# Planning of two sparse layers in fewer operations, with a subtraction moved to GpSimd and gathers issued in pairs

## The reference

```python
def _L1_ffn_ref(x, Wr, W1, b1, W2, b2):
    DIM, E, K, H = (256, 8, 2, 1024)
    x_flat = x.reshape(-1, dim)
    logits = x_flat @ Wr
    w, ind = jax.lax.top_k(logits, K)
    w = jax.nn.softmax(w, axis=-1)
    combine = jnp.einsum('tke,tk->te', jax.nn.one_hot(ind, E, dtype=x.dtype), w)
    def body(acc, params):
        W1e, b1e, W2e, b2e, ce = params
        h = jax.nn.gelu(x_flat @ W1e + b1e, approximate=False)
        y = h @ W2e + b2e
        return (acc + ce[:, None] * y, None)
```

## Time and profile before

| | us |
|---|---|
| median of three runs | 1571.42 (1568.8 to 1572.77) |
| profiled execution, whole | 1568.99 |
| its span, first to last instruction | 1567.2 |
| PE busy | 1324.8 (85%) |
| DVE busy | 962.4 (61%) |
| ACT busy | 860.1 (55%) |
| POOL busy | 708.6 (45%) |
| mean granted PE clock | 0.927 of full |
| first sparse layer, from the planning to its last tile | about 519 to 818 |
| second sparse layer | about 1029 to 1239 |

### The profile page before, as it was taken

One profiled execution on the slowest core, in us unless ns is written; L12 is line 12 of the kernel. 1 busy time (PEld: TensorE's weight loads), 2 busy tenths in 40 slices (PEclk: granted clock), 3 DMA queues, 4 the chain that ended last, 5 costly groups with the idle time before them and its releaser, 6 DMA issues.

```text
span 1567.2 us, 29388 instructions
## 1 busy us (share of the span) xinstructions
PE 1324.8 (85%) x9497; PEld 962.0 (61%) x9524; DVE 962.4 (61%) x2651; ACT 860.1 (55%) x1718; POOL 708.6 (45%) x835
## 2 busy tenths in 40 slices
PE   2899899997998499999999699849999388995985
PEld 1455489854566289999986366627887245664343
DVE  6789653426785643333338499575554277967787
ACT  2366854434786245555535388535554155885554
POOL 4567330105632577767641473158994415622000
PEclk9999999997899699999999699969999797997998
DMA  9997030179640333343248974024444498710001
GB/s 291 280 159 145 2 98 0 37 226 194 120 77 15 101 124 120 116 158 112 79 146 275 213 135 84 13 86 151 146 135 162 150 277 166 138 33 1 0 14 41
DMA packets 115441, 188.86 MB, mean 121 GB/s; under 512 B 21169, under 2 KB 91441, under 8 KB 109105
## 3 DMA queue, kind: packets, MB, share of 16 engines
q0 software_dynamic: 36928, 105.19, 28.2%
q1 hardware_dynamic: 78368, 81.79, 16.9%
HBM read 128.17 MB, written 50.20 MB: 114 GB/s over the span
## 4 chain that ended last, share of the span: by engine, by line
PE 67%; DVE 14%; DMA 7%; ACT 6%; issue 4%; POOL 1%; ACTq 0%; SPq 0%; DVEq 0%; POOLq 0%
PE PS L1196 10%; PE PS L1216 10%; PE PS L1037 9%; PE PS L992 8%; PE PS L996 3%; PE PS L1208 3%; PE PS L1074 2%; DMA qk_parts<-q_parts 2%; PE PS L1010 2%; PE PS L878 2%; PE PS L1050 2%; PE PS L1017 2%; DMA stack<-qk_parts 1%; DVE act L2577 1%; PE PS L864 1%
## 5 line engine op out<-in xcount | busy, mean ns | idle before, releaser
L2092 DVE TENSOR_REDUCE nm<-PS 128x2 f32<-128x512 f32 x384 | 250.3, 676 | 42.6 <-PE PS L992 41.4
L992 PE MATMUL PS<-stack 48*128 48x256 f32 x1024 | 215.8, 336 | 43.6 <-DVE nm L2092 10.6
L992 PEld LDWEIGHTS PS<-stack 48*128 48x128 f32 x1024 | 154.5, 208 | 128.5 <-issue 59.1
L996 PE MATMUL PS<-stack 49*128 49x256 f32 x1024 | 206.0, 325 | 0.9 <-ACT probs L1517 0.6
L1216 PE MATMUL PS<-weights,hh 128*128 x936 | 190.0, 292 | 3.9 <-DVE hl L2419 3.7
L1196 PE MATMUL PS<-weights,xh 128*128 x468 | 171.1, 420 | 10.7 <-DVE xl L2403 5.2
L667 POOL DMA_DIRECT2D stack<-mt x128 | 72.8, 569 | 213.8 <-ACT mt L1526 211.8
L1517 ACT ACTIVATE probs<-PS 128x512 f32<-128x512 f32 x256 | 145.1, 595 | 42.9 <-PE PS L996 16.7
L1517 ACT ACTIVATE xng<-PS 128x512 f32<-128x512 f32 x256 | 145.2, 595 | 24.3 <-PE PS L1017 13.8
L1216 PEld LDWEIGHTS PS<-weights,hh 128*128 128x128 f32 x936 | 152.8, 193 | 6.3 <-issue 5.8
L996 PEld LDWEIGHTS PS<-stack 49*128 49x128 f32 x1024 | 145.5, 198 | 10.1 <-ACT probs L1517 4.3
(11 more groups left out here) (329 smaller groups left out, 3073.3 us busy)
## 6 DMA issues: line engine op xcount, KB each, us to landing
stack<-qk_parts POOLq DMA_DIRECT2D x128, 256.0 KB, 4.2
qk_parts<-stack SPq DMA_DIRECT2D x32, 512.0 KB, 6.9
qk_parts<-q_parts SPq DMA_DIRECT2D x32, 512.0 KB, 10.8
stack<-qk_parts POOLq DMA_DIRECT2D x128, 128.0 KB, 3.8
weights<-W_dram POOLq DMA_DIRECT2D x12, 1024.0 KB, 7.2
wide<-ctxT_dram SPq DMA_DIRECT2D x16, 512.0 KB, 8.1
wslot<-y_tokens SPq DMA_DIRECT2D x16, 512.0 KB, 7.6
weights<-W_dram POOLq DMA_DIRECT2D x12, 512.0 KB, 5.1
```

The costliest lines, as they stand in the source:

```text
L992: mm = pe.matmul(PS[:, u % 3, to], nat_q[:, at], nat_k, start=True, stop=True)
L996: mm = pe.matmul(PS[:, 3 + v % 3, to], key_k[:, at], key_q, start=(l > 0 or half == 0), stop=(l > 0), skip_group_check=(l == 0))
L2092: nc.vector.tensor_reduce(nm[:, j % 2, at:at + 2], PS[:, (2 * t + h) % 3, :].rearrange("p (q n) -> p q n", q=2), AX.X, ALU.max, negate=Tru ...
```

## The change

It makes five edits, in both sparse layers.

1. The two compares into `eq` become one over both choices, and so do the two multiplications by `where` and the two sums into `posf`. The semaphore counts (ROUTE + 2, PLANNED = 50) follow.
2. The eight chained operations on `tile_e` become one compare into `begun` (128 x 39 x 8, in the memory of `late`) and one sum over the eight experts.
3. `rows_of_tiles` is cut into `rows_from`, which writes `idx`, and `rows_to`, which writes `into`. For the first eight tiles `rows_to` is called after the tables.
4. The four pieces of `split_low(l, 1, q)` leave DVE. POOL does the same subtractions after its normalising and before it waits for `xt_out` and `idx_done`. Its last one adds to `split_done`.
5. Of the first eight gathers, 2 and 3 wait for the landing of 0 and 1; 4 waits for 2 and 3, and 6 for 4 and 5.

```diff
@@ gpsimd
                         normalise(2 * h)
                         normalise(2 * h + 1)
+                    for q in range(CUTS):
+                        at = slice(q * n // CUTS, (q + 1) * n // CUTS)
+                        pool.wait_ge(split_hi, SPLITS * (l - 1) + CUTS + q + 1)
+                        ins = nc.gpsimd.tensor_tensor(w_lo(l, 1)[:, at], w_raw(l, 1)[:, at], w_hi(l, 1)[:, at].bitcast(F32), ALU.subtract)
+                    pool.wait_ge(split_done, EXPERTS * (l - 1) + 1)
+                    ins.then_inc(split_done, 1)
                     pool.wait_ge(xt_out, 16 * GROUPS * l)
                     pool.wait_ge(idx_done, 2 * l - 1)
                     for i in range(AHEAD):
+                        if 2 <= i < 4:
+                            pool.wait_ge(xq_in[i - 2], 16 * l)
+                        elif i >= 4 and i % 2 == 0:
+                            pool.wait_ge(xq_in[i // 2], 32 * l)
                         gather(i, tile_in(i, i % 2)).then_inc(xq_in[i if i < 2 else 1 + i // 2], 16)
@@ tensor
-                pe.wait_ge(route_v[l], ROUTE + 3)
+                pe.wait_ge(route_v[l], ROUTE + 2)
@@ vector
-            def rows_of_tiles(l, k, first, part, block):
+            def rows_from(l, k, first, part, block):
...
                 nc.vector.scalar_tensor_tensor(idx[:, at], block, float(P), tmp(1), ALU.mult, ALU.add).then_inc(idx_done, 1)
+                return k + 2
+
+            def rows_to(l, k, first, part, block):
+
+                n = part.shape[1]
+                at = slice(first, first + n)
+                tmp = lambda r: scan[:, 0].rearrange("p t e -> p (t e)")[:, 32 * (r + 1):32 * (r + 1) + n]
                 nc.vector.scalar_tensor_tensor(tmp(2), block, 0.5, pad_row[:, at], ALU.is_lt, ALU.mult).then_inc(route_v[l], 1)
-                dve.wait_ge(route_v[l], k + 3)
-                tt(tmp(0), part, tmp(2), ALU.add).then_inc(route_v[l], 1)
-                dve.wait_ge(route_v[l], k + 4)
+                dve.wait_ge(route_v[l], k + 1)
+                nc.vector.tensor_tensor(tmp(0), part, tmp(2), ALU.add).then_inc(route_v[l], 1)
+                dve.wait_ge(route_v[l], k + 2)
                 nc.vector.scalar_tensor_tensor(into[:, at], block, float(P), tmp(0), ALU.mult, ALU.add).then_inc(placed, 1)
-                return k + 4
+                return k + 2
...
-                for m in range(2):
-                    nc.vector.tensor_tensor(eq[:, m], iotas[:, 0:8].unsqueeze(1).broadcast_to([P, TILES, 8]),
-                                            gt[:, m, :].unsqueeze(2).broadcast_to([P, TILES, 8]), ALU.is_equal
-                                            ).then_inc(route_v[l], 1)
-                k += 2
-                dve.wait_ge(route_v[l], k)
+                choices = eq[:].rearrange("p m t e -> p (m t) e")
+                then(tt(choices, iotas[:, 0:8].unsqueeze(1).broadcast_to([P, 2 * TILES, 8]),
+                        gt[:, 0:2, :].rearrange("p m t -> p (m t)").unsqueeze(2).broadcast_to([P, 2 * TILES, 8]), ALU.is_equal))
                 then(tt(picked[:], eq[:, 0], eq[:, 1], ALU.add))
...
-                for m in range(2):
-                    then(tt(eq[:, m], eq[:, m], where, ALU.mult))
-                    then(nc.vector.tensor_reduce(posf[:, m, :], eq[:, m], AX.X, ALU.add))
+                then(tt(eq[:], eq[:], where.unsqueeze(1).broadcast_to([P, 2, TILES, 8]), ALU.mult))
+                then(nc.vector.tensor_reduce(posf[:].rearrange("p m t -> p (m t)"), choices, AX.X, ALU.add))
...
-                k = rows_of_tiles(l, k, 0, PS[:, 6, 0:AHEAD], PS[:, 6, AHEAD:2 * AHEAD])
-                for e in range(8):
-                    if e == 0:
-                        then(ts(tile_e[:, 0, :], iotas[:, 0:NT], escan[:, es, 0:1], None, ALU.is_ge))
-                    else:
-                        then(nc.vector.scalar_tensor_tensor(tile_e[:, e % 2, :], iotas[:, 0:NT], escan[:, es, e:e + 1],
-                                                            tile_e[:, 1 - e % 2, :], ALU.is_ge, ALU.add))
+                k = rows_from(l, k, 0, PS[:, 6, 0:AHEAD], PS[:, 6, AHEAD:2 * AHEAD])
+                begun = late[:].rearrange("p i d -> p (i d)")[:, 0:8 * NT].rearrange("p (n e) -> p n e", e=8)
+                then(tt(begun, iotas[:, 0:NT].unsqueeze(2).broadcast_to([P, NT, 8]),
+                        upto.unsqueeze(1).broadcast_to([P, NT, 8]), ALU.is_ge))
+                then(nc.vector.tensor_reduce(tile_e[:, 1, :], begun, AX.X, ALU.add))
...
                 ts(upto_e[:], upto[0:1], 1.0 + (NT + 1) * (l - 1), None, ALU.add).then_inc(tables, 1)
+                k = rows_to(l, k, 0, PS[:, 6, 0:AHEAD], PS[:, 6, AHEAD:2 * AHEAD])
...
-                rows_of_tiles(l, k, AHEAD, PS[:, 7, 0:rest], PS[:, 7, rest:2 * rest])
+                k = rows_from(l, k, AHEAD, PS[:, 7, 0:rest], PS[:, 7, rest:2 * rest])
+                rows_to(l, k, AHEAD, PS[:, 7, 0:rest], PS[:, 7, rest:2 * rest])
...
                 plan_late(l)
-                for q in range(CUTS):
-                    split_low(l, 1, q)
                 a(1, 1)
```

More of the change, by code:

```diff
@@ L70 @@
 ROUTE = 17
-PLANNED = 59
+PLANNED = 50
 BY_GROUP = (0, 4, 6)
@@ L2297, in plan @@
                     ts(pad_row[:], iotas[:, 2 * TILES + 1:2 * TILES + 1 + NT], float(P), col("part"), ALU.mult, ALU.add)
-                for m in range(2):
-                    nc.vector.tensor_tensor(eq[:, m], iotas[:, 0:8].unsqueeze(1).broadcast_to([P, TILES, 8]),
-                                            gt[:, m, :].unsqueeze(2).broadcast_to([P, TILES, 8]), ALU.is_equal
-                                            ).then_inc(route_v[l], 1)
-                k += 2
-                dve.wait_ge(route_v[l], k)
+                choices = eq[:].rearrange("p m t e -> p (m t) e")
+                then(tt(choices, iotas[:, 0:8].unsqueeze(1).broadcast_to([P, 2 * TILES, 8]),
+                        gt[:, 0:2, :].rearrange("p m t -> p (m t)").unsqueeze(2).broadcast_to([P, 2 * TILES, 8]), ALU.is_equal))
                 then(tt(picked[:], eq[:, 0], eq[:, 1], ALU.add))
-                assert k == ROUTE + 3
+                assert k == ROUTE + 2
                 total, where = scan[:, 0, 0, :], scan[:, 1]
```

## The result

| | before | after |
|---|---|---|
| median of 17 runs each, us | 1572.4 | 1581.24 |
| ratio, 95% interval | | 1.0059 (1.0043 to 1.0074), or +9.3 us (6.8 to 11.6) |
| profiled execution, whole | 1568.99 | 1581.19 |

The change makes the kernel slower by 0.6%. Single executions of one kernel lie up to some 20 us apart, so a difference of a few us needs many runs, or a look into the traces. To compare traces I cut out of each the two *legs*: from the first operation of the planning (the compare into `eq`) to the start of the last scatter, in layer 1 and in layer 2. Outside them all kernels of this text have the same code, except where an experiment says otherwise.

The account below looks back on a forecast made before the run. Layer 1 was taken to be bounded by PE's start, layer 2 by POOL's fetch of expert 2. Layer 1's +0.6 (+3.0 - 2.4) and layer 2's +5.2 gave +5.8 us, 1577.2 on the median, range 1568 to 1582.

Parts of the forecast that it names:

- the forecast's own case: Both sparse layers: POOL's subtractions and DVE's planning lock each other out in turns; +5.8 us, 1577.2, range 1574 to 1580, chance 0.50.
- Fewer operations before `idx`: DVE's planning ahead of the row numbers: merged multiplies, sums and compares save 0.65 us in layer 1, 0.7 in layer 2.
- Tables 1.8 sooner after `idx`: DVE's planning: one compare and one sum of 0.48 us each, and `into` moved behind, bring the tile tables 1.8 us sooner.
- DVE and POOL take turns by operations: Planning: one engine waits out the other's operation, then runs at its own length; gather 0 near 541 in layer 1, +3.2 in layer 2.
- DVE waits out all: Rival, chance 0.13: DVE's planning waits out all of POOL's subtractions; layer 1 +3.3, layer 2 +5.9, sum +9.2, 1580.6.
- b(1) +3.0, its clock -2.4: PE, layer 1: tile 1's first product starts 3.0 us later, but a shorter gap keeps the clock up, 2.4 back; net +0.6.
- Pairs: 15.8 us for eight gathers: POOL's queue: gathers two at a time wait for landings, so eight end after 15.8 us, 5.1 more than now.
- Fetch of layer 2 +5.2: POOL in layer 2: late gather 0 and the pairs put the fetch of expert 2 at 1066.6 for 1061.39, +5.2 us.
- All of it reaches the end of layer 2: POOL has no slack behind its fetch of expert 2, so the whole +5.2 us reaches the end of the layer.
- taken up behind it: Rival, chance 0.12: the scatters' stalls absorb POOL's lateness in layer 2, which costs nothing; sum about +0.6, 1572.0.
- no locking: Rival, chance 0.18: POOL's subtractions and DVE's planning each run at own pace; layer 1 -4.2, layer 2 +1.3, sum -2.9, 1568.5.
- faster outright: Rival, chance 0.05: no locking, and pairs land at once so POOL's layer 2 fetch gains 2.4 us; sum -6.6, 1564.8.

Follow-up runs that it names:

- e1: Changed kernel with the four subtractions of expert 1 back on DVE behind plan_late, gathers still paired; -5.3 us (-9.3 to -1.4) against the kernel before.
- e3: Kernel before with edits 1 to 3 only: subtractions on DVE as before, gathers not paired; -7.4 us (-11.3 to -3.3) against the kernel before.
- e5: e3 with the four subtractions on POOL but earlier, two ahead of each half of the normalising; -8.6 us (-12.4 to -4.7) against the kernel before.
- e6: Changed kernel with POOL waiting for DVE's row_of before its four subtractions; one run, only the trace read: legs +4.8 and +3.2 us against the kernel before.
- e2: Changed kernel without the waits that pair the gathers, subtractions still on POOL; +7.4 us (2.5 to 12.1) against the kernel before.
- e9: Changed kernel with each POOL subtraction waiting until the one before is done; one run, only the trace read: legs +3.1 and +0.9 us against before.
- e7: Changed kernel with POOL's four subtractions cut into 32 small ones; one run, only the trace read: legs +9.0 and +3.6 us against before.
- e12: e4 with paired gathers and POOL's layer 1 fetch of expert 2 held until ACT wrote tile 1's first half of hh; one run, legs -0.8, -3.2 us against before.
- e4: e3 with the four subtractions on DVE earlier, in its idle gaps while the attention output is added; -12.7 us (-17.9 to -7.7) against the kernel before.
- e11: The e4 kernel unchanged, timed a second time; -10.5 us (-16.0 to -5.0) against the kernel before.

## Why the prediction was right, and where it was off

The forecast was 1577.2 with a range of 1568 to 1582; measured are 1581.24, inside it but outside the 1574 to 1580 that the forecast's own case was given. The sign, the mechanism and the place (POOL's subtractions against DVE, POOL's queue in layer 2) were right; one step was wrong, and its rival was what happened. The two layers came out the other way round: I had +0.6 and +5.2 and the legs say +4.7 and +3.3. Layer 1's miss and layer 2's have opposite signs, so the sum is nearer than its parts, and that is luck.

- *Fewer operations before `idx`, 0.65 and 0.7.* Sum and multiply over 256 took 0.42 each, as assumed. But `in_row` started 0.04 us sooner in layer 1 in e1, 0.6 later in e3, and 1.7 sooner in layer 2 in both. What I had not seen: the chain of small operations runs beside POOL's normalising, and one of 0.17 us takes up to 0.64 there, as this one of layer 2 in the trace of before:

```profile
523.90 0.17 DVE L2321 TENSOR_SCALAR escan<-escan 128x8 f32<-128x8 f32 x1
...
1035.63 0.64 DVE L2321 TENSOR_SCALAR escan<-escan 128x8 f32<-128x8 f32 x1
```

In layer 2 the gain is the same in every trace (`in_row` 9.39 us into the planning in the two with the old operations, 7.67 to 7.70 in all with the new ones but e5's 8.42), and as much as that lies in operations that no edit touched, from the first sum `scan` to the last on `escan`: 4.97 us before, 3.28 in e3. I take it that they meet the normalising at other moments; no run shows that alone. In layer 1 it differs from trace to trace (7.58 and 7.86 old; 7.53 to 8.73 new, where the subtractions hold nothing up). Edits 1 to 3 by themselves are worth 4.7 us by e3's medians, 7.4 by its ratio and 5.0 by its legs, of which 2.7 are not shown to be theirs; my sum had 1.4.
- *Tables 1.8 sooner after `idx`.* 4.15 us before, 2.25 after: 1.9. Compare and sum took 0.47 and 0.48 for my 0.48.
- *DVE and POOL take turns by operations (+3.2 at gather 0 in layer 2, gather 0 near 541 in layer 1).* This is the step that failed. DVE waited out all four subtractions in both layers; gather 0 went at 544.25, and in layer 2 at 20.50 us into the planning for 17.17: +3.33, near my +3.2 only by luck: the lock cost 5.0 where I had 3.9 (3.2 + 0.7), and the fewer operations gave 1.7 where I had 0.7. The rival "DVE waits out all", to which I gave 0.13, is the case, at 1580.6, with +3.3 and +5.9 for the layers. Its layer 2 is too high as well (and by the steps of my own sum +4.2 at gather 0 would be +6.2 at the fetch). Row 3.52 us in the earlier trace rows had said so: a DVE operation begun during the first of two subtractions waited out both. I preferred rows 9, which are of single operations that meet. The Trainium skill ("SBUF — State Buffer", section "SBUF: two separate sides") states that whichever starts first keeps the ports "for the whole instruction"; the 6.56 us of e6 agree. `tile_of`, which has one SBUF input in f32, is held too. What follows when GpSimd's operations queue up is told by the 10.05 and 14.00 us: a waiting DVE can be passed over four and 30 times.
- *b(1) +3.0, its clock -2.4.* Counted from the planning's start, b(1) came 5.96 us later (39.68 for 33.72), by the lock; it took 3.03 us, 2.45 less, at a granted clock of 1.00 (2.4 GHz) from 555 to 559. The clock term held. 5.96 - 2.45 = 3.5, the rival's +3.3. No term of mine covered the stall ahead of `hh` of tile 1, 5.44 us idle for 2.91:

```profile
568.03 1.09 ACT L1693 ACTIVATE hh<-PS 128x512 fp32r<-128x512 f32 x2 [5.44 <-remote]
```

b(1)'s end came 3.5 us later and the start of the last second product 4.6; in e2, which has the same lock and no stall (2.88), it was 4.8 and 4.2. So the stall is the likely source of the rest, and no run of the changed kernel takes it away.
- *Pairs: 15.8 us for eight gathers.* 14.1 and 14.3. Gather 2 went 3.1 us after gather 0 (forecast 3.6), gather 4 7.3 (8.6), gather 6 11.9 and 12.1 (13.7). The landing of a pair and the wake behind it held POOL 2.0 to 2.6 us after the second issue; I had counted 2.8 + 0.84 from its start. Against 10.7 that is +3.6 for +5.1.
- *Fetch of layer 2 +5.2.* Measured +3.6. POOL's wait for the splits (2.36 us) is gone, as forecast, and so is the one for the late `idx` (1.03): 3.3 by gather 0 and 3.6 by the pairs, less the two, is 3.6. The 1.6 that I had too much are nearly all the size of the pairs, 15.8 for 14.3. The wait for the late `idx` behind the gathers, 2.15 to 2.20 us in e2 and e3, is why beside e2 the pairs moved the fetch by 1.95 us only (33.48 to 35.43): they fill that wait first.
- *All of it reaches the end of layer 2.* +3.6 at the fetch, +3.3 at the last scatter. From the fetch to the last scatter the fourteen traces take 175.7 to 178.5 us (177.7 before, 177.5 changed), with no relation to how late the fetch comes. The rival "taken up behind it" falls.
- The rivals *no locking* and *faster outright* fall with the 10.05 us.

The sum, 5.8 by the forecast, is 8.0 by the two legs (9.2 with the slow last product of before at its usual length) and 9.3 by the timing.

## What to carry to other kernels

Work that one engine does back to back beside another's serial chain must be priced as a block, not operation by operation; where the two took turns here (e6, e9), the chain came out within 0.8 us of the block's price in layer 1. Put GpSimd's elementwise work where DVE has none that matters, or put it into DVE's own idle gaps: with that, and without the pairs, a change of +9.3 us became one of -10.5 to -12.7. When a step is taken off one queue, look for the second wait behind the first (here the late `idx` behind the splits). Of a bundle of edits, time the parts: here one that gains 2 to 7 us, one that costs over 10 and one that costs up to 4 went in together.

## What the hardware showed that was not expected

- Back-to-back GpSimd subtractions passed over a waiting DVE operation for 10.05 us (four of 2.3 us) and 14.00 us (30 of 0.44 us); with a gap of 0.15 us between them, DVE got in each time. What decides at the border of two operations without a gap is open: in e6 a border in the middle of the block let DVE in, in e7 the border ahead of the first small piece in layer 2, in the changed kernel none.
- It works the other way too: a GpSimd subtraction took 6.51 us for 2.35, and eight normalising operations 14.41 for 9.9, beside `in_row`'s 4.42.
- ACT stood idle up to 3 us longer than its data asked for (5.60 for 2.65) while the DMA engines were full of a 1 MB load, released by something that the profile doesn't name: 9.08 to 9.18 us after the load's issue in six traces, and the stall moved with the load (e12). DVE's like one (4.10 for 2.02 in e4) fell into gathers that kept the DMA engines under half busy; its cause is open.
- Two executions of the same kernel, on two chips (e4, e11), had legs 5.3 us apart, as much as a single edit here is worth. That the chip makes it is not shown: e4's execution was the slowest of its eight, 1568.37 for a median of 1559.43, and the medians of the two are 2 us apart.
